# Edge scores: the exponential of a quarter four entries earlier, and one small exponential ahead of the scores

## The reference

```python
Xq = (H @ W_lin.T).reshape(bt, n, h, dh)
Qs = Xq[:, src]
Kt = Xq[:, dst]
e = jnp.einsum('behd,hd->beh', jax.nn.leaky_relu(Qs + Kt, LRELU_SLOPE), a)
e = e + jnp.log(A0[src, dst] + EPS)[None, :, None]
e_t = e.transpose(1, 0, 2)
m = jax.ops.segment_max(e_t, src, num_segments=n)
ex = jnp.exp(e_t - m[src])
denom = jax.ops.segment_sum(ex, src, num_segments=n)
attn = ex / denom[src]
```

## Time and profile before

| | |
|---|---|
| median of 3 runs | 1859.08 us (1858.97 to 1859.26) |
| profiled execution, its own time | 1856.83 us |
| its span | 1855.1 us |
| TensorE busy | 1790.5 us, 13191 matmuls |
| VectorE busy | 1464.2 us, 3954 instructions |
| ScalarE busy | 1100.4 us, 1763 instructions |
| GpSimd busy | 579.4 us, 1625 instructions |
| edge scores, first gather to the start of the last dots | 1464.40 to 1599.84 us |
| table loads of ScalarE in the whole span | 4 |

### The profile page before, as it was taken

The page is one execution under the profiler, slowest core; times in us unless marked ns, Lnnn a source line. Parts: engine busy times, 40 slices in busy tenths (PEclk is TensorE's granted clock), DMA queues, the critical chain, the costliest instruction groups (busy, mean ns, idle before and its releaser), DMA issues. The chain is left out here.

```text
span 1855.1 us, 35420 instructions
## 1 busy us (share of the span) xinstructions
PE 1790.5 (97%) x13191; PEld 1459.1 (79%) x13191; DVE 1464.2 (79%) x3954; ACT 1100.4 (59%) x1763; POOL 579.4 (31%) x1625
## 2 busy tenths in 40 slices
PE   7999999999999999999999999999889999999997
PEld 6777878888899999988887777877678644588875
DVE  7888875666656767878888888988778788798876
ACT  5555565454445545554444436767667799766676
POOL 3454521232233443000000004446644200104655
PEclk9999999999999999999999999999999999999999
DMA  4112000001000000010000005312222310003223
GB/s 134 32 35 70 1 24 23 1 1 46 1 1 1 1 1 1 1 46 1 1 1 1 1 19 170 126 47 93 89 69 72 112 40 29 12 1 104 82 81 104
DMA packets 63417, 77.76 MB, mean 42 GB/s; under 512 B 3975, under 2 KB 55437, under 8 KB 63245
## 3 DMA queue, kind: packets, MB, share of 16 engines
q1 hardware_dynamic: 62380, 72.35, 12.0%
q0 software_dynamic: 864, 3.15, 0.5%
HBM read 47.17 MB, written 28.31 MB: 41 GB/s over the span
## 5 line engine op out<-in xcount | busy, mean ns | idle before, releaser
L2213 ACT ACTIVATE l_gates<-l_acc,l_b 128x512 f32<-128x512 f32 (+1 forms) x408 | 240.0, 620 | 84.5 <-PE l_acc L480 82.3
L478 PE MATMUL l_acc<-l_x_hi,l_w1x_hi 128*128 128x336 f32 (+1 forms) x544 | 188.2, 346 | 1.1 <-ACT l_gates L2213 0.8
L480 PE MATMUL l_acc<-l_x_lo,l_w1x_hi 128*128 128x336 f32 (+1 forms) x544 | 187.6, 345 | 0.0
L479 PE MATMUL l_acc<-l_x_hi,l_w1x_lo 128*128 128x336 f32 (+1 forms) x544 | 187.2, 344 | 0.0
L2102 ACT ACTIVATE l_x_hi<-hT 128x512 fp32r<-128x512 f32 (+1 forms) x112 | 82.4, 787 | 173.6 <-PE l_acc L480 173.6
L478 PE MATMUL l_acc<-l_x_hi,l_w0x_hi 128*128 128x512 f32 x464 | 181.4, 391 | 3.3 <-ACT l_gates L2213 3.3
L479 PE MATMUL l_acc<-l_x_hi,l_w0x_lo 128*128 128x512 f32 x464 | 180.6, 389 | 0.0
L480 PE MATMUL l_acc<-l_x_lo,l_w0x_hi 128*128 128x512 f32 x464 | 180.6, 389 | 0.0
L2223 ACT ACTIVATE l_gates<-l_cell 128x512 f32<-128x512 f32 (+1 forms) x112 | 63.7, 569 | 168.2 <-DVE l_cell L2274 138.6
L249 POOL TENSOR_TENSOR bi_shifted<-bi_shifted 32x126 f32<-32x126 f32 (+61 forms) x62 | 18.0, 290 | 390.8 <-DVE bi_shifted L236 390.8
L478 PE MATMUL l_acc<-l_h_hi,l_w0h_hi 128*128 128x512 f32 x320 | 124.7, 390 | 0.7 <-DVE l_h_lo L2291 0.7
(11 more groups left out here) (547 smaller groups left out, 5358.0 us busy)
## 6 DMA issues: line engine op xcount, KB each, us to landing
xin<-in_x_t SPq DMA_DIRECT2D x16, 512.0 KB, 3.7
hidB<-in_x SPq DMA_DIRECT2D x16, 512.0 KB, 5.0
x<-hT SPq DMA_DIRECT2D x16, 512.0 KB, 3.2
hidB<-x SPq DMA_DIRECT2D x16, 512.0 KB, 3.8
x<-hidB SPq DMA_DIRECT2D x16, 512.0 KB, 2.9
attention_residual<-x SPq DMA_DIRECT2D x16, 512.0 KB, 3.9
out_x<-hT SPq DMA_DIRECT2D x16, 512.0 KB, 2.9
l_rawx<-in_wih SPq DMA_DIRECT2D x4, 1024.0 KB, 5.5
```

The lines of the kernel that those rows point to most:

```text
L478: t.matmul(out, left[0], right[0], start=start, stop=False)
L479: t.matmul(out, left[1], right[0], start=False, stop=False)
L480: return t.matmul(out, left[0], right[1], start=False, stop=stop)
L2213: i = a.activation(gates[:, j, q, 0:n], acc[:, j, q, 0:n], FUNC[q], bias=b[:, o:o + 1])
```

## The change

A new tile `exp_table` of 128x8 is added to the constants, the first tiles that are placed. In the projections' loop on ScalarE, at the end of the turn g = LAST − 1 = 14, that is behind the split of group 15, an exponential of eight columns of the tile of ones is written into it; nobody reads it. In the scores, a quarter's exponential follows the leaky step of entry 8 of the next quarter in place of entry 12: entries 40, 72 and 104 in place of 44, 76 and 108.

```diff
@@ constants
-    return dict(ident=sb("ident", [P, P]), ones=sb("ones", [P, P]), adj_t2=sb("adj_t2", [P, P]), adj2=sb("adj2", [P, P]))
+    return dict(ident=sb("ident", [P, P]), ones=sb("ones", [P, P]), adj_t2=sb("adj_t2", [P, P]), adj2=sb("adj2", [P, P]),
+                exp_table=sb("exp_table", [P, 8]))
@@ convolution_and_projections, on_scalar
                 if 6 <= g + 4 < GROUPS:
                     output_scaled(g + 4)
+                if g == LAST - 1:
+                    a.activation(c["exp_table"][:, :], c["ones"][:, 0:8], ACT.Exp)
             queries(LAST)
@@ edge_attention, on_scalar
                 q, at = b // PER_Q - 1, b % PER_Q
-                if q >= 0 and at == 12:
+                if q >= 0 and at == 8:
                     exponent(q)
```

## The result

The changed kernel takes 1855.0 us (median of 15 runs, 1853.58 to 1858.63), the kernel before, beside it, 1858.61 us (15 runs, 1857.27 to 1863.75). The ratio is 0.9981, with a 95% interval of 0.9974 to 0.9987: faster by 3.5 us, with an interval of 2.4 to 4.8 us. The forecast was 1855.3 us.

A forecast was written before the change was run, and what follows sets the result against it. TensorE was taken to bound the score stage. Gains of 1.42 (load), 2.22 (stack waits) and 0.18 us (smaller lateness) sum to 3.82 us, taking the median from 1859.08 to 1855.3 us; range 1854.4 to 1856.9 us.

The forecast's parts named there:

- The bound: Edge-score stage, 1464 to 1600 us: the chain of waits was said to pass almost wholly on TensorE.
- the prediction's second term: TensorE's wait for the stack of entry 60 and its later-quarter counterparts goes: 0.74 us each, 2.22 us in three quarters.
- Part 1: Small exponential ahead of the scores: costs nothing in ScalarE's pause and removes the load after entry 44, 1.42 us.
- no shift of the first gather at 1464.40: Sign expected in the profile after: the scores' first gather on TensorE still starts at 1464.40 us.
- Part 2: Exponential after entry 8, not 12: no new wait, 0.21 us kept per quarter; stack waits go, 2.22 and 0.18 us gained.
- the turn: Dots step where weights are turned: of 5.18 us, 0.74 us is stack wait, 0.42 us transposes; about 4.44 us stays.
- The spare time: Stack of entry 60 on VectorE: forecast done 1.1 us before TensorE wants it.
- The load back in the scores: Rival: table load placed again at the first leaky step or entry 40; gain 2.40 us, 1856.7 us, chance 0.06.
- The overrun: Rival: load and small activation overrun ScalarE's pause, scores begin 1.0 us later; 1856.3 us, chance 0.04.
- VectorE staying late: Rival: VectorE's gain is lost in other waits, only the load's 1.42 us come; 1857.7 or 1856.8 us, chance 0.07.
- The waiting exponential: Rival: after entries 40, 72, 104 the moved exponential waits for L1474, paid in full; over 1859.1 us, chance 0.02.
- The tile: Rival: the new tile shifts all others by 32 bytes per partition; sign open, chance 0.03, half of it slower.

The follow-up runs named there:

- the run after entry 4: The changed kernel with each of the first three quarters' exponentials after entry 4 in place of 8; ratio 1.0024 to the kernel before, first to last dots 134.06 us.

## Why the prediction was right, point by point

**The bound.** Right for the kernel after: from 1470.95 to 1595.43 us its chain of waits has gathers, dots and turns alone. For the kernel before, "almost wholly on TensorE" was read too far. Its chain leaves TensorE for the load, and three times more for VectorE, in the second quarter for 14.5 us (start us, us, engine, tile, line):

```profile
1545.93 1.23 DVE hidB L1478
...
1559.68 0.70 DVE stack L1458
1560.42 0.74 PE sc_g L1560 x2
```

It begins at the sum that waited for the exponential and ends at the gather that waited for its stack. This is the path on which the prediction's second term rests, so the sum isn't touched; the sentence that what only holds another engine counts for nothing is.

**Part 1.** The small activation takes 0.21 us (0.2 forecast), the pair 1.5 us, its cost is nothing. The removed load gives 1.42 us as forecast (5.65 to 4.23 us); alone it gave 1.46 us from the first to the last dots. That the table outlives the block's edge is shown: the kernel has four loads as before, the last now at L981, and none at L1423. The sign "no shift of the first gather at 1464.40" holds against the split only; counted from the start of the span that gather is at 1465.76 us, since the changed kernel is 1.35 us late by then. The two pauses are 1.82 + 1.79 = 3.61 us, not the prediction's "up to 3.4 us"; nothing hangs on it.

**Part 2.** No new wait at entry 8, 0.21 us for the exponential at its new place (4.23 and 4.24 us), the 0.05 to 0.08 us of earlier stacks gone. The term that was mis-sized is the turn: the transposes were put at 0.42 us, the wait for the stack at 0.74 us and the step that stays at 4.44 us. The step measures 4.35 us, so the transposes add 0.33 us to it and the wait was 0.83 us. From the transposes to the dots are 1.47 us in both profiles (1527.20 to 1528.67, now 1526.22 to 1527.69), so the difference is ahead of them: I had counted a gather at 0.27 us also behind the wait, and there the two gathers took 0.58 us (1526.62 to 1527.20), where four take 1.03 us now (1525.19 to 1526.22). Three times 0.09 us are the 0.27 us between the forecast 3.82 and the measured 4.09 us.

**The spare time.** For the stack of entry 60 1.1 us were left by the forecast, worked out with the second quarter's gain. In the profile after it isn't waited for in any quarter. In the second quarter the stack is done at 1556.98 + 0.69 = 1557.67 us. It is first needed by the third of the gathers that begin at 1558.10 us, 0.26 us apart, so about 0.95 us is left.

**The rivals.** The load back in the scores: no. The overrun: no; 3.0 us of loads and small activations still delayed nothing. VectorE staying late: no; the move alone gives 2.64 us in the stage, so this rival is out. The waiting exponential: not at entry 8, but its price is as stated, in full, and at entry 4 it makes the kernel slower than before. The tile: nothing.

**The whole.** The forecast was 1855.3 us, measured are 1855.0 us. The stage's 4.09 us lie inside the interval of the whole (3.5 us, 2.4 to 4.8), and more agreement than that isn't shown. That the two times meet to 0.3 us is in part luck: the stage gave 0.27 us more than forecast, the kernel before has 1858.61 us in 15 runs where the forecast started from 1859.08 us in three, and a part of the gain is lost to the clock, about 1 us by the estimate above (0.9915 against 0.9925), which the prediction had not in its sum. In every series the kernels with the small exponential, the move or both have a mean clock below that of the kernel before beside them (0.9908 to 0.9916 against 0.9925, 0.9911 and 0.9915 against 0.9921). Whether the change draws these stretches or only shifts the work against them was not tried, nor what places a stretch in one execution and not in the next. Whether the load's part alone shortens the whole time isn't shown by the ratio of its runs, and only by the estimate at equal clock; the stage is shorter, by its steps.

## What to carry to other kernels

A wait on an engine that isn't the bound can still be on the path if the same engine builds something for the bound later in its list: look at how late it is at its next due item, not at how long it waits. Here a wait of 3.96 us and one of 1.76 us cost TensorE the same 0.83 us. When an item is moved forward in an in-order queue, compare the end of its input with the end of what stands before it at the new place; a wait there can be paid in full by all that is behind, as it was after entry 4. And measure a change of some tenths of a per cent by the steps of its stage too, since stretches of a lower clock, as in this case, can hide it in the whole time.

## What the runs showed of the hardware that was not expected

Single stretches at TensorE's lower level (3.4 us in ten, a granted clock of 0.83) appear in some executions and not in others at places where nothing was changed. The one at 1740 us cost 1.40 us and the one inside the scores of the run after entry 4 went with 1.34 us, while the one at 1030 us cost nothing that can be seen.

Four gathers, four transposes and four gathers one after another without a wait take 0.33 us more than eight gathers (4.35 against 4.02 us a step). Two gathers behind an idle time of TensorE took 0.58 us to the next start, where four without one take 1.03 us.

A load of ScalarE's table and an activation of 128x8 repeat after 1.50 us (1.28 and 0.21 us, two and four times in turn), and the load starts as soon as the activation ahead of it has ended (1459.53 and 1459.54 us).
